# Three engine loops turned at different places, layer 0 norm work reordered, and experts split around the norm transposes

## The reference, cut to what matters

```python
for W, a_s, a_d, bg, R, g, b in layers:              # 3 layers
    h = _gat(x, src, dst, W, a_s, a_d, bg)           # alpha-weighted sum over the chain's neighbours
    x = gelu(_layer_norm(h + x @ R, g, b))
h = _layer_norm(x.reshape(B, T, J * 64) @ fpW + fpb) # "fp" projection
h = concatenate([h, txt], axis=1)
h = h + attention(layernorm(h))      # only output 0: q = l2norm(silu(conv(silu(x wq1) wq2))), mem_w1, mem_w2, w_out
h = h + experts(layernorm(h))        # router softmax, top 2 of 8; expert: gelu(x w1 + b1) w2 + b2
```

## Time and profile before

| | us |
|---|---|
| median of 3 runs | 4956.21 (4944.56 to 4972.84) |
| the profiled execution's own time | 4948.98 |
| its span | 4947.1 |
| PE busy in the span | 4335.2 (88%) |
| DVE busy | 3554.3 (72%) |
| ACT busy | 2606.4 (53%) |
| POOL busy | 628.8 (13%) |
| PE's granted clock, mean | 0.958 of full |

### The profile page before, as it was taken

One profiled execution on the slowest core, in us unless ns is written; L12 is line 12 of the kernel. 1 busy time (PEld: TensorE's weight loads), 2 busy tenths in 40 slices (PEclk: granted clock), 3 DMA queues, 4 the chain that ended last, 5 costly groups with the idle time before them and its releaser, 6 DMA issues.

```text
span 4947.1 us, 73345 instructions
## 1 busy us (share of the span) xinstructions
PE 4335.2 (88%) x23014; PEld 1946.6 (39%) x23014; DVE 3554.3 (72%) x8027; ACT 2606.4 (53%) x3945; POOL 628.8 (13%) x746
## 2 busy tenths in 40 slices
PE   3788989988898988999988899998889898898988
PEld 3223333433434344343433434344343433434345
DVE  1677777777777777777877777777777787777762
ACT  0454645555564555555555564555555555565643
POOL 1111101111120111102011120111102011110100
PEclk9898999999999999999999999999999999999998
DMA  2000000000000000000000000000000000000000
GB/s 93 2 1 3 1 3 4 3 4 1 6 1 3 3 2 5 1 3 3 3 3 1 6 1 3 3 2 5 1 3 3 3 3 2 5 1 3 3 2 5
DMA packets 23087, 25.64 MB, mean 5 GB/s; under 512 B 3395, under 2 KB 21835, under 8 KB 22139
## 3 DMA queue, kind: packets, MB, share of 16 engines
q1 hardware_dynamic: 22650, 20.26, 1.3%
HBM read 16.06 MB, written 4.19 MB: 4 GB/s over the span
## 4 chain that ended last, share of the span: by engine, by line
PE 59%; DVE 23%; issue 10%; ACT 6%; DVEq 1%; SPq 0%; DMA 0%; POOL 0%; ACTq 0%; POOLq 0%
PE bank L859 9%; PE bank L921 7%; PE bank L912 7%; PE bank L812 6%; PE bank L770 4%; PE bank L696 4%; PE bank L829 3%; ACT X L1244 2%; PE bank L850 2%; PE bank L815 2%; DVE X L1852 2%; DVE TB L1820 2%; DVE rt L1770 2%; PE bank L612 1%; PE bank L832 1%
## 5 line engine op out<-in xcount | busy, mean ns | idle before, releaser
L1288 ACT ACTIVATE X<-bank,bgc 128x512 f32<-128x512 f32 (+1 forms) x624 | 418.4, 671 | 478.4 <-PE bank L859 478.4
L1244 ACT ACTIVATE X<-X,c_vec 128x1024 f32<-128x1024 f32 (+2 forms) x432 | 492.2, 1172 | 287.2 <-DVE X L1852 286.7
L1852 DVE TENSOR_TENSOR X<-X,bank 128x1024 f32<-128x1024 f32 (+2 forms) x432 | 480.7, 1138 | 198.8 <-PE bank L736 119.8
L912 PE MATMUL bank<-XT,c_w 128*128 128x512 f32 x1024 | 495.0, 612 | 22.0 <-ACT SQ L1324 21.4
L812 PE MATMUL bank<-R,c_W 64*128 64x512 f32 (+1 forms) x832 | 479.1, 657 | 31.1 <-issue 24.5
L921 PEld LDWEIGHTS bank<-c_w,SQ 128*128 128x128 f32 x4096 | 476.2, 192 | 43.2 <-issue 39.2
L921 PE MATMUL bank<-c_w,SQ 128*128 128x128 f32 x4096 | 482.8, 276 | 0.0
L846 PE MATMUL bank<-X,WR 64*128 64x512 f32 (+1 forms) x832 | 473.6, 650 | 0.0
L859 PE MATMUL bank<-R,c_C 128*128 128x512 f32 (+1 forms) x832 | 471.2, 649 | 0.0
L532 POOL TENSOR_TENSOR R<-X 128x512 f32<-128x512 f32 (+1 forms) x208 | 257.0, 1239 | 1653.6 <-PE bank L812 873.3
L1272 ACT ACTIVATE R<-bank 128x512 f32<-128x512 f32 (+1 forms) x416 | 241.7, 581 | 355.0 <-PE bank L812 223.1
(11 more groups left out here) (259 smaller groups left out, 6870.6 us busy)
## 6 DMA issues: line engine op xcount, KB each, us to landing
c_w<-in_w SPq DMA_DIRECT2D x2, 2048.0 KB
out<-Ho SPq DMA_DIRECT2D x32, 128.0 KB, 2.7
c_fpW<-in_fpW SPq DMA_DIRECT2D x1, 3200.0 KB
X<-in_x SPq DMA_DIRECT2D x34, 75.0 KB, 2.6
X<-in_txt SPq DMA_DIRECT2D x32, 64.0 KB, 1.8
X<-in_chain SPq DMA_DIRECT2D x1, 1300.0 KB
X<-in_sel SPq DMA_DIRECT2D x1, 600.0 KB
X<-in_sel SPq DMA_DIRECT2D x1, 300.0 KB
```

The lines of the kernel that those rows point to most:

```text
L912: mm(hidden_bank(e, m), w1[:, k * P:k * P + P], XT2[:], start=True, stop=True).then_inc(hid_ps, 1)
L1244: A_(dst, dst, ACT.Gelu, bias=v(f"b{l}"), scale=v(f"g{l}")).then_inc(x_ok, 1)
L1288: A_(dst, bZ[k % 2][:, 0:cols], ACT.Identity, bias=bias).then_inc(zs_ok, 1)
L1852: TT(dst, dst, b, ALU.mult).then_inc(u_ok, 1)
```

## The change

Five things change together. First, the loop bodies are cut elsewhere. PE's turns round between layer 1 and layer 2, while ACT's turns just ahead of the last two pose transposes before `window`, and DVE's turns at the beginning of `window`. POOL's and SP's stay. Work that stood inside the loop once is now also written out ahead of it or behind it. Second, in a layer with the chain `own` of tasks 0 and 1 is issued behind `product_d(2)` instead of ahead of their `plus_neighbours`. Third, in `window` all of layer 0's products, sums of squares and their transpose come before the token's transposes, and `rstd` comes before `query_silu`. Fourth, an expert's `down` (for expert 5 also its `up`) is cut in pieces that stand on both sides of `rstd_rows`, most `keep_warm` products there go, and DVE adds the expert behind the second `normalise` instead of ahead of the first. Experts 0, 4 and 5 get PSUM bank 5 in place of 3. Fifth, the top-two routing parts on DVE stand at every second task of layer 1 (10, 12, to 20) instead of at six in a row (10 to 15), and `add_expert(t, 3)` stands ahead of `alphas_out`.

```diff
-            return (3, 4, 6, 7, 3, 3, 4, 3)[e]
+            return (5, 4, 6, 7, 5, 5, 4, 3)[e]
...
     graph_layer on PE
...
-                    if n == lag and l == 1 and moe:
-                        added(s - 2, 7)
+                        if n == 1:
+                            if l == 1 and moe:
+                                added(s - 2, 7)
+                            own(s, l, 0)
+                            own(s, l, 1)
                     if lag <= n < NT[l] + lag:
-                        own(s, l, n - lag)
+                        if n >= 4 or not chain:
+                            own(s, l, n - lag)
                         plus_neighbours(s, l, n - lag, chain)
...
+            def hidden_done(t, e):
+
+                pe.wait_ge(hid_sb, t * E * MT + e * MT + MT + 1)
...
     window on PE
...
-                        if n == 11 and tail:
-                            pe.wait_ge(h_ok, t + 1)
-                            columns_of(Xn, bank[1])
...
+                    variance(w, 0, BATCHES[0] - 1)
+                    variance_rows(w, 0)
+                if tail:
                     pe.wait_ge(h_ok, t + 1)
                     columns_of(Xn, bank[1])
-                if tail:
                     pe.wait_ge(xt_sb, t * 2 + 1)
                     mm(bank[2][:], wq1[:], XT[:], start=True, stop=True).then_inc(q1_ps, 1)
+                if moe:
+                    up(t - 1, 5, (0, 1))
                 if main:
-                    variance(w, 0, BATCHES[0] - 1)
-                    variance_rows(w, 0)
+                    if not moe:
+                        keep_warm(8, bank[3])
+                    rstd_rows(w, 0)
                 if tail:
                     pe.wait_ge(q1_sb, t + 1)
                     mm(bank[1][:], wq2[:], Q1, start=True, stop=True).then_inc(q2_ps, 1)
                 if moe:
-                    up(t - 1, 5)
-                    down(t - 1, 5)
+                    up(t - 1, 5, (2, 3))
+                    if not main:
+                        down(t - 1, 5)
...
                 for m in range(PAIRS[0] + 2) if main else ():
-                    if moe and m in (2, 3):
-                        keep_warm(5 - m, bank[4])
+                    if moe and m == 1:
+                        down(t - 1, 5, (0, 1))
+                        hidden_done(t - 1, 5)
+                    if moe and m == 2:
+                        down(t - 1, 5, (2, 3))
...
     layer 1 on PE (layer 2 likewise, with expert 4)
...
                     up(t, 0)
-                    down(t, 0)
+                    down(t, 0, (0, 1))
                 else:
                     keep_warm(18, bank[3])
                 rstd_rows(s, 1)
-                keep_warm(3, bank[4])
+                if tail:
+                    down(t, 0, (2,))
+                    hidden_done(t, 0)
                 pe.wait_ge(rp_ok, s * 3 + 2)
                 for m in range(PAIRS[1] + 2):
+                    if m == 2 and tail:
+                        down(t, 0, (3,))
                     if m in (2, 3):
-                        keep_warm(5 - m, bank[4])
+                        keep_warm(2, bank[4])
                     if m < PAIRS[1]:
                         spread_rstd(s, 1, m)
-                    if tail and m == 2:
+                    if tail and m == 3:
                         added(t, 0)
...
-                iteration(0, False, False, True)
+                layer_1(0, False, False)
+                layer_2(0, False, True)
+                layer_1(1, True, False)
                 with pe.Fori(1, STEPS - 1) as s:
-                    iteration(s, True, True, True)
-                iteration(STEPS - 1, True, True, False)
+                    layer_2(s, True, True)
+                    layer_1(s + 1, True, True)
+                layer_2(STEPS - 1, True, False)
...
     ACT
...
+                between(1, False)
+                iteration(1, True, True)
+                with act.Fori(2, STEPS - 1) as s:
+                    between(s, True)
                     iteration(s, True, True)
...
     DVE
...
                 if tail:
                     pose_token(t)
-                    query_silu(t)
                 if main:
                     rstd(w, 0)
                 if tail:
+                    query_silu(t)
                     convolve(t)
-                if moe:
+                if moe and not main:
                     add_expert(t - 1, 5)
                 for m in range(PAIRS[0]) if main else ():
                     normalise(w, 0, m)
+                    if m == 1 and moe:
+                        add_expert(t - 1, 5)
...
-                    if moe and 10 <= n < 16:
-                        top_two(t, n - 10)
+                    if moe and 10 <= n <= 20 and n % 2 == 0:
+                        top_two(t, (n - 10) // 2)
...
                 for m in range(PAIRS[1]):
                     normalise(s, 1, m)
+                    if moe and m == 1:
+                        add_expert(t, 0)
...
+                with dve.Fori(2, STEPS - 1) as s:
+                    links[0], start[0] = 0, s * LINKS + (first - 2 * LINKS)
+                    window(s, True, True, True)
                     iteration(s, True, True)
```

More of the change, by code:

```diff
@@ L1108, in iteration @@
                     up(t, 4)
-                    down(t, 4)
+                    down(t, 4, (0, 1))
                 else:
@@ L1112, in iteration @@
                 rstd_rows(s, 2)
-                keep_warm(3, bank[4])
+                if tail:
+                    down(t, 4, (2,))
+                    hidden_done(t, 4)
                 pe.wait_ge(rp_ok, s * 3 + 3)
@@ L1116, in iteration @@
                     if m == 2:
-                        keep_warm(3, bank[4])
+                        if tail:
+                            down(t, 4, (3,))
+                        keep_warm(2, bank[4])
                     if m == 3:
@@ L1355, in window @@
                         .then_inc(q2_sb, 1)
-                if main:
-                    A_(carrier[:, 2:3], mhalf[:], ACT.Gelu)
                 if moe:
-                    hidden(t - 1, 5)
-                if main:
-                    rstd_out(w, 0)
+                    hidden(t - 1, 5, (2, 3))
                 if tail:
@@ L2102, in iteration @@
                 rstd(s, 2)
-                if moe:
-                    add_expert(t, 4)
                 for m in range(PAIRS[2]):
                     normalise(s, 2, m)
+                    if moe and m == 1:
+                        add_expert(t, 4)
                     if nxt and m < 4:
                         coordinates_by_parts(m)
-                window(s + 1, nxt, True, moe)
             def experts(t):
```

77 lines of the change are left out of this document (39 added, 38 removed).

## The result

The changed kernel takes 4893.91 us (median of 4 runs, 4876.22 to 4905.46) beside 4950.39 us of the kernel before on the same chip: ratio 0.988, interval 0.983 to 0.992. In a later comparison it took 4909.08, ratio 0.990 (0.987 to 0.994). The forecast was 4800, with a range up to 4890. The sign was right, the gain less than half of what was forecast. The profiled execution took 4905.46 us, its granted clock was 0.949 (before 0.958). The step stands at its limit of 292 and the clock above 0.94.

A forecast was written before the change was run, and what follows sets the result against it. PE was taken as the main bound (59% of the chain). Terms of 18 us (turn), 42 (window) and 89 (the others), 149 in all, from 4949 gave 4800; likeliest range 4735 to 4865, eight in ten 4715 to 4890.

The forecast's parts named there:

- Turn: Loop turns of PE, DVE and ACT: moving them to where engines wait wins 1.3 us a step, bounds -0.5 to +2.1.
- the dip: Half clock on PE that idle time at its moved turn may bring: costs 1.6 us, half of it charged.
- Rival B: Turns at separate places make other engines wait once each: turn term falls to -2.0 us a step, 4846 us, chance 0.12.
- `own` ahead: Starts of layers 1 and 2: the two `own` products fill PE's wait for DVE, +1.5 and +0.1 us a step.
- Routing parts: Layer 1: spreading the top-two parts on DVE removes PE's wait of 1.40 to 1.43 us, +1.7 us a step.
- the table load: ACT's load of 1.28 us, now ahead of the routing's exponential inside layer 1: 0.5 us charged against the routing gain.
- Norms: Norms of layers 1 and 2: splitting `down` lets PE transpose the factors earlier, +1.4 and +1.2 us a step.
- Window: Window: earlier `rstd` brings the score transposes forward, +3.0 us a step, bounds +1.0 to +5.0, 2.0 left at half clock.
- Rival C: PE falls to 1.2 GHz behind the norm transposes and its turn: mean clock 0.93 or less cancels the gain, chance 0.05.

The follow-up runs named there:

- f2: Changed kernel with PE's, ACT's and DVE's loops turning at their old places, and eight products ahead of PE's loop to shift its head: 4883.16 us, ratio 0.982.
- g2: Changed kernel with `own` of tasks 0 and 1 of layers 1 and 2 issued as before: 4868.85 us, ratio 0.983.
- g1: Changed kernel with PE's turn back at its old place, loop head shifted, and six `keep_warm` products in the window: 4834.15 us, again 4823.76.
- h1: g1 with `own` of tasks 0 and 1 issued as before: 4821.09 us, again 4821.63.
- e4: Changed kernel with two `keep_warm` products ahead of each of spreads 3, 4 and 5 of the window, six in all: 4877.77 us, ratio 0.985.
- f3: Changed kernel with PE's loop turning inside layer 1, ahead of the third spread, where PE waits for DVE: 4869.43 us, ratio 0.982.
- f1: Changed kernel with only PE's turn back between window and layer 1, and eight products ahead of PE's loop to shift its head: 4871.89 us, ratio 0.982.
- e1: Changed kernel with only PE's turn back between window and layer 1, loop head not shifted: 4912.31 us, ratio 0.992.

## Why the prediction was too low, step by step

*Turn (+1.3 a step, 18 us): wrong, and here the sum broke.* "The turn thus costs 2.8 us" came from comparing steps and was about right for all three at one place: 1.8 us are won ahead of the first product and 0.9 up to task 3, `own`'s part included. DVE's and ACT's new places are hidden, as said: at both the engine still waits for PE behind the turn (4.70 us on DVE, 0.91 on ACT). The step that failed is "There 1.87 - 1.18 = 0.7 us stay exposed". A turn lasts 3.3 to 4.0 us in PE's stream in these two kernels, 1.87 was what showed behind 2.00 us of queued products, and at the new place only 0.5 us of products were queued. The idle time grew by 1.9 us instead of 0.7, the dip that I charged at 0.8 cost 1.1 up to layer 2's first spread, and 1.0 more at task 5. Rival B had this mechanism ("DVE's may be longer"), but for the wrong engine, and its price was close: it puts the moved turns at -2.0 us a step, 28 us, and f2 says 11 to 26 by the times and 27 to 39 by the ratios. So instead of +18 us the term is -11 or worse.

*`own` ahead (+1.5 and +0.1): wrong, 0 or a loss.* "As the idle time is mostly gone" was the error. The third spread still comes 7.2 us behind the step's first product, when DVE's first tile is done. At its place the new order wins 0.4 us up to task 3 in the changed kernel (g2 stands at 19.1) and loses 0.5 in g1 (h1 stands at 18.0).

*Routing parts (+1.7): right in mechanism,* 2.6 by the table, near the high bound. The charge of 0.5 for the table load did not show.

*Norms (+1.4, +1.2): right at their place* (about 1.1 where the clock held, 0.5 in the changed kernel, and 1.3), and mostly or wholly lost again, with more half clock later in the step.

*Window (+3.0): right as a mechanism, and in this kernel cancelled.* DVE's first multiplication comes 3.6 us earlier where I had worked out 5.7 (2497.57 to 2492), since the wait of `convolve` for the second query product was not in the working. What I had put in one sentence ("At half clock 2.0 us are left") was the case that came, all of the row up to the transposes at 0.50, and then nothing was left (-0.4).

*The clock.* Rival C named the place and the sign of this loss. Its limit, a mean clock of 0.93 in the step, was not reached, so it was no slower kernel, but 6.6 us more of PE's work a step at the half clock are 3.3 us, or 46 us in 14 steps, about half of the 94 us between 4800 and 4894. That is an estimate, as if all of this work were on the path to the end. Keeping the clock up at the window's end alone (e4) won 16 to 31 us. I had charged the clock at single waits (0.8 us at the turn) and given a fall that is carried on to other stages no share in the sum.

## What to carry to other kernels

A loop turn's length is read from the branch in the engine's stream, not from the gap behind the last product: put the turn where much queued work stands ahead of it. A wait for another engine behind it did not help by itself: f3 had one and was no better than f1. And look whether the loop's head lies close ahead of an instruction block's end. When idle time is taken out of one place, look at the granted clock everywhere in the step before counting the gain, and test each part alone and as the last one undone: here the window was worth 34 us alone and 47 to 64 as the last part, and `own` ahead nothing in g1 and a loss of 21 to 40 in the changed kernel.

## What the hardware showed that I had not expected

- A backward turn costs 3.3 to 4.0 us on PE in all 26 turns of the loops of the kernel before and the changed one, up to 5.3 in the experiments' traces (f3), and 2.8 to 3.1 us on DVE in the kernel before, from the branch to the next instruction. A branch that is not taken, at the loop's end, took 0.08 us on PE. The Trainium skill's page Advanced Engine Details and Errata gives about 108 ns for a compare and branch in its section Control Flow Timing. The trace agrees with that for the branch that is not taken, and for no turn of PE.
- Sixteen instructions ahead of a loop, executed once, are worth 40 us of 4912 (e1 against f1). With them the second stop behind the turn, while a second block of instructions comes in, is gone from all 12 turns.
- With the norms' `keep_warm` and idle time back, the half clock in a step fell from 27.6 to 18.8 us, most of it in the window, 24 us and more behind the norm's transpose back. Which of the two does it is not shown.
